# A state-space mixer and a LoRA feed-forward on one core: tiles of x and of turned rows wait for the products of their own place, and the first drive is made in halves

## The reference, cut to what matters

```python
proj = x @ W_in.T;  u, gate = split(proj)
u = silu(causal_conv4(u) + conv_b)
dt, B, C = split(u @ Wx.T);  dt, B, C = rmsnorm(each)
delta = softplus(dt @ Wdt.T + dt_bias)
state = exp(delta_t * A) * state + (delta_t * u_t) * B_t   # over t
y = sum_n(state * C_t) + u * D;   y = y * silu(gate)
x1 = layernorm(x + y @ W_out.T)
out = layernorm(x1 + x1 @ W.T + b + picked_lora(x1))
```

## Time and profile before

| what | before |
|---|---|
| median of 3 runs | 2262.96 us (2259.63 to 2263.5) |
| profiled execution, its own time | 2262.3 us |
| its span | 2260.5 us |
| TensorE busy | 2064.6 us, 91% |
| VectorE busy | 1994.2 us, 88% |
| GpSimd busy | 1819.4 us, 80% |
| ScalarE busy | 1481.8 us, 66% |
| granted TensorE clock, mean | 0.967 |

### The profile page before, as it was taken

The page is one execution under the profiler, slowest core; times in us unless marked ns, Lnnn a source line. Parts: engine busy times, 40 slices in busy tenths (PEclk is TensorE's granted clock), DMA queues, the critical chain, the costliest instruction groups (busy, mean ns, idle before and its releaser), DMA issues. The chain is left out here.

```text
span 2260.5 us, 30748 instructions
## 1 busy us (share of the span) xinstructions
PE 2064.6 (91%) x10528; PEld 1548.8 (69%) x10528; DVE 1994.2 (88%) x2403; ACT 1481.8 (66%) x2197; POOL 1819.4 (80%) x780
## 2 busy tenths in 40 slices
PE   8989689999999799999899997989989999897998
PEld 6867567777565477777775556868866556675577
DVE  4438899999999999999999999989989999999933
ACT  4478667777666677676886567675686566856521
POOL 4379888987999999778799988977688987699740
PEclk9989899999999999999999998999999999998999
DMA  4467556765332447655453333474453337443340
GB/s 153 137 214 238 198 199 232 226 206 181 92 119 82 131 148 234 233 190 166 137 190 113 111 97 97 152 261 154 148 181 115 108 94 224 154 156 127 102 141 38
DMA packets 168764, 354.84 MB, mean 157 GB/s; under 512 B 18656, under 2 KB 45408, under 8 KB 168608
## 3 DMA queue, kind: packets, MB, share of 16 engines
q1 hardware_dynamic: 168608, 352.87, 48.7%
HBM read 283.96 MB, written 68.85 MB: 156 GB/s over the span
## 5 line engine op out<-in xcount | busy, mean ns | idle before, releaser
L1544 POOL TENSOR_TENSOR drive<-delta_u,b_bcast 128x2048 f32<-128x2048 f32 x256 | 1172.1, 4582 | 106.9 <-PE state_t L916 98.7
L1098 DVE TENSOR_TENSOR_SCAN drive<-decay,drive 128x512 f32<-128x512 f32 x1024 | 1191.5, 1204 | 60.1 <-ACT decay L1338 34.7
L1338 ACT ACTIVATE decay<-delta,a_sb 128x512 f32<-128x512 f32 x1024 | 694.8, 688 | 416.0 <-DVE drive L1098 411.2
L916 PEld LDWEIGHTS state_t<-identity,drive 128*128 128x128 f32 x4096 | 485.5, 145 | 337.6 <-DVE drive L1098 148.6
L916 PE MATMUL state_t<-identity,drive 128*128 128x128 f32 x4096 | 592.1, 283 | 130.0 <-DVE drive L1098 96.1
L1106 DVE SCALAR_TENSOR_TENSOR y_acc<-state_t,c_rows,y_acc 128x512 f32<-128x512 f32 x724 | 513.2, 734 | 44.4 <-PE state_t L916 40.2
L947 PE MATMUL bank<-cols_high,w_split 128*128 128x512 f32 (+1 forms) x1240 | 523.5, 422 | 20.8 <-POOL w_split L1569 8.5
L949 PE MATMUL bank<-cols_high,w_split 128*128 128x512 f32 (+1 forms) x1240 | 491.0, 396 | 0.0
L948 PE MATMUL bank<-cols_low,w_split 128*128 128x512 f32 (+1 forms) x1240 | 489.0, 394 | 0.0
L970 PE MATMUL bank<-channels,w_raw 128*128 128x512 f32 x896 | 424.2, 597 | 1.3 <-POOL channels L1565 0.9
L1549 POOL TENSOR_TENSOR y_acc<-y_acc,scaled 128x512 f32<-128x512 f32 x236 | 303.0, 1284 | 120.6 <-ACT scaled L1358 118.8
(11 more groups left out here) (224 smaller groups left out, 1446.9 us busy)
## 6 DMA issues: line engine op xcount, KB each, us to landing
w_split<-w_split SPq DMA_DIRECT2D x272, 512.0 KB, 4.0
b_bcast<-b_rows SPq DMA_DIRECT2D x256, 256.0 KB, 3.5
w_raw<-in_w_out SPq DMA_DIRECT2D x112, 256.0 KB, 3.0
w_raw<-in_w_in SPq DMA_DIRECT2D x96, 256.0 KB, 4.3
gates<-scratch SPq DMA_DIRECT2D x64, 256.0 KB, 3.9
scratch<-gates SPq DMA_DIRECT2D x64, 256.0 KB, 4.7
rows<-in_x_rows SPq DMA_DIRECT2D x4, 2048.0 KB, 9.5
out<-rows SPq DMA_DIRECT2D x16, 512.0 KB, 4.6
```

The lines of the kernel that those rows point to most:

```text
L916: last = engine.transpose(bank[0:tile.shape[1], i * P:(i + 1) * P], tile, identity[:, :])
L1098: engine.tensor_tensor_scan(state, decay[(GT * s + t) % DECAYS][:, :], state, 0.0, ALU.mult, ALU.add).then_inc(signal["scan"])
L1338: engine.activation(decay[i % DECAYS][:, :], delta[:, g % 2, t, :], ACT.Exp, scale=a_sb[:, j, n:n + 1]).then_inc(signal["decay"])
L1544: engine.tensor_tensor(drive[key % DRIVES][:, :, :], du[:, :, :], row, ALU.mult).then_inc(signal["drive"])
```

## The change

It does four things. `products(b, k)` asks for place k of the 32 jobs alone, and `x1_job`, `load_x` and the waits of ScalarE use it with the tile's own k; for sequences 2 and 3 `x_high` needs `f_mm` of its own k in all eight jobs and, newly, `route_mm` of that k. The assumed duration of `x_first` in `load_x(1)` goes from 0.69 to 1.3 us. Drive 0 is made by two instructions of two tiles, `drive_begun` after the first half of `du`, `drive` after the second, and the scans of tiles 0 and 1 of unit 0 wait for the first of them alone. Everything else of the program is as before, but for the order that the plan gives.

```diff
+def drive_of(s, t):
+    return "drive" if s or t >= GT // 2 else "drive_begun", s
-    def products(b):
-        return [(stage, (b, j, HT - 1)) for stage in ("u_mm", "g_mm") for j in range(DT)]
+    def products(b, k):
+        return [(stage, (b, j, k)) for stage in ("u_mm", "g_mm") for j in range(DT)]
...
-        old = products(s + 1)
+        old = products(s + 1, h)
...
     def load_x(b, due):
-        old = [("f_mm", (b - 2, h, HT - 1)) for h in range(HT)] if b > 1 else products(0) if b else []
         for k in range(HT):
+            old = [("f_mm", (b - 2, h, k)) for h in range(HT)] + [("route_mm", (b - 2, 0, k))] if b > 1 else products(0, k) if b else []
...
-            put("POOL" if b > 1 else "DVE", due + 0.1 * k, 1.28 if b > 1 else 0.69, *low_of(b, k), [("x_high", (b, k))],
+            put("POOL" if b > 1 else "DVE", due + 0.1 * k, 1.28 if b > 1 else 1.3, *low_of(b, k), [("x_high", (b, k))],
...
-        put("POOL", q - 8, 4.56, "drive", s, [("fetch", s), ("du", (b, g, 1))] + (
+        if s == 0:
+            put("POOL", q - 8.2, 2.35, "drive_begun", s, [("fetch", s), ("du", (b, g, 0)), ("lora_rest", 0)] + [("x_first", (0, k)) for k in range(HT)])
+        put("POOL", q - 8, 4.56 if s else 2.35, "drive", s, [("fetch", s), ("du", (b, g, 1))] + ([] if s else [("drive_begun", 0)]) + (
...
-            put("DVE", i, 1.13, "scan", (s, t), [("drive", s), ("decay", (s, t))],
+            put("DVE", i, 1.13, "scan", (s, t), [drive_of(s, t), ("decay", (s, t))],
...
-                    e.wait_ge(*done("drive", s))
+                    e.wait_ge(*done(*drive_of(s, t)))
...
-                            e.wait_ge(*done("f_mm", (b - 2, h, HT - 1)))
+                            e.wait_ge(*done("f_mm", (b - 2, h, k)))
+                        e.wait_ge(*done("route_mm", (b - 2, 0, k)))
                     if b == 1:
-                        products_done(0)
+                        products_done(0, k)
...
-                    products_done(s + 1)
+                    products_done(s + 1, h)
...
-                if stage == "drive":
+                if stage in ("drive", "drive_begun"):
                     b, g, n = UNITS[key]
+                    tiles = slice(0, GT // 2) if stage == "drive_begun" else slice(0 if key else GT // 2, GT)
...
-                    e.wait_ge(*done("du", (b, g, 1)))
+                    e.wait_ge(*done("du", (b, g, 0 if stage == "drive_begun" else 1)))
...
-                    engine.tensor_tensor(drive[key % DRIVES][:, :, :], du[:, :, :], row, ALU.mult).then_inc(signal["drive"])
+                    engine.tensor_tensor(drive[key % DRIVES][:, tiles, :], du[:, tiles, :], row, ALU.mult).then_inc(signal[stage])
```

More of the change, by code:

```diff
@@ L1323, in scratch_of, with products_done @@
                 return scratch[place["scratch", holder]]
[L1325 to L1328, removed]
+            def products_done(b, k):
+                for stage in ("u_mm", "g_mm"):
+                    for j in range(DT):
+                        e.wait_ge(*done(stage, (b, j, k)))
             for _, stage, key in plan.work["ACT"]:
@@ L1531, in _ @@
             for _, stage, key in plan.work["POOL"]:
-                if stage == "drive":
+                if stage in ("drive", "drive_begun"):
                     b, g, n = UNITS[key]
-                    row = b_bcast[key % 2][:, :].unsqueeze(1).broadcast_to([P, GT, T])
+                    tiles = slice(0, GT // 2) if stage == "drive_begun" else slice(0 if key else GT // 2, GT)
+                    row = b_bcast[key % 2][:, :].unsqueeze(1).broadcast_to([P, tiles.stop - tiles.start, T])
                     e.wait_ge(*done("fetch", key))
-                    e.wait_ge(*done("du", (b, g, 1)))
+                    e.wait_ge(*done("du", (b, g, 0 if stage == "drive_begun" else 1)))
                     if key >= DRIVES:
```

## The result

The changed kernel takes 2271.73 us, the median of 7 runs (2269.09 to 2275.12); the kernel before, in runs beside it, 2262.32 (2259.63 to 2265.76). The ratio is 1.0043 with a 95% interval of 1.0033 to 1.0052: **9.4 us slower**. The profiled execution took 2273.07 us with a span of 2271.3, at a mean granted clock of 0.962 (before: 0.967).

What follows compares the result with a forecast made beforehand. VectorE and GpSimd set the pace up to 682 us, both nearly together with TensorE up to 1186, then TensorE. Terms -1.5 + 0 - 2 - 3 + 0 = -6.5 us gave 2255.8, as median 2256.5 us; range 2241 to 2272.

Steps and rivals of the forecast that it cites:

- the sum: Whole kernel: -1.5 + 0 - 2 - 3 + 0 = -6.5 us on the profiled 2262.3 us.
- moves only the order: Plan's price of x of sequence 1's low parts, now 1.3 us: said to change just the order; no term given.
- the low parts' new place: VectorE's eight low parts of x of sequence 1, moved earlier: 0 taken, between -8.2 and +17.3 us.
- Part one: First drive in halves at the start: drive 1 gains 0.7 to 2 us, 1.5 us carried to the end.
- Part two: x of sequence 1, waits by place: first product 4 to 8 us earlier, but 0 at the end.
- the first u product: Sign for sequence 1 on TensorE: starts at 295 to 299 us if the forecast is right.
- the first `x_high`: Sign for x of sequence 1: comes before 256 us if the forecast is right.
- The release at 682.26: Start of sequence 0's second-half output products: 1 to 2 us earlier; a move over 4 us means wrong.
- Part three: x of sequences 2 and 3, waits by place: gains of 2 us (0 to 2.2) and 3 us (0 to 6).
- Part four: Turned rows, waits by place: TensorE still runs the due products first; nothing gained, at best 2 us.
- The nearest rival: TensorE after 1186 us: a turn of states gets in front of ready products, +7.2 us, 2270 us; chance 0.16.
- The other slower rival: x of sequence 1: all eight low parts under drives, by the lock, +10.8 us, 2274 us; chance 0.07.

Runs made afterwards that it cites:

- e6: All edits of the changed kernel, queues in the order of the kernel before, first half drive put in by hand: 2259.18 us, ratio 0.9989.
- e5: Kernel before with only the assumed duration of a low part of x of sequence 1 at 1.3 instead of 0.69 us: 2268.95 us, ratio 1.0031.
- e12: Kernel before with the assumed duration of a low part of x of sequence 1 at 0.70 instead of 0.69 us: 2280.25 us, ratio 1.0075.
- e9: All edits of the changed kernel, queues in the order it gets without the half drive, half drive put in by hand: 2254.04 us, ratio 0.9963.
- e7: Kernel before with only the first drive in halves, put in by hand, order else that of before: 2259.88 us, ratio 0.9993.
- e2: Kernel before with only the first drive in halves, in the new order the plan gives: 2265.11 us, ratio 1.0010.
- e3: Kernel before with only the waits by place for x of sequences 2 and 3, in its own order: 2258.88 us, ratio 0.9981.
- e10: Kernel before with the assumed duration at 1.3 us and the pair of delta products behind sequence 0's turned rows: 2261.89 us, ratio 0.9998.
- e1: Changed kernel with one need more, putting the pair of delta products behind the turned rows of sequence 0: 2267.11 us, ratio 1.0019.

## Why the prediction was wrong

I forecast 2256.5 us and a gain; it is 2271.7 and a loss. The edits, taken by themselves, did roughly what the steps said or less; the failure is one assumption under all of them.

- **The step that failed** is in the sum: it has no term for the new order. I wrote that the price "moves only the order", as if that were nothing, took 0 for the low parts' new place, and priced every edit in the order of before. The queues are the output of `Plan.arrange`, and the new order is the largest term of all. In the order of before the edits gain 2.7 us (e6), in the one that the plan draws for them they lose 9.4, so this draw costs 12.1 us where I had put 0. The price alone, with no edit at all, costs 7.1 us (e5) and a hundredth of a microsecond 17.6 (e12), and another draw for the same edits gains 8.6 (e9).
- **Part one** (-1.5): the half drive's length was right, 2.40 us for 2.38. I had placed it in GpSimd's gap of 2.68 us; the plan put it behind du, and drive 1 gained 0.1 us. Put in the gap by hand it gives 1.2 us at drive 1 and 2.0 at the end, not told apart from none (e7). With its own order it costs 2.2 (e2). In the kernel after, the stretch from the first half of du to unit 4 even grew by 1.7 us.
- **Part two** (0): the first u product came at 299.71 us (I said 295 to 299), the first `x_high` at 259.2 (I said before 256); counted from unit 4 the u product is only 1.9 us earlier, where I had 4 to 8. The release at 682.26 moved by +6.6 us to 688.86, past the 4 us that I had named as the sign of an error. That what TensorE gains there is lost before 682 holds for TensorE alone; but the same place can move VectorE's recurrence either way: 7.8 us later at unit 16 in the kernel after, 5.5 earlier in e9.
- **Part three** (-2 and -3): near in sum, and partly by luck. Alone it gives 4.0 us (e3), none of it at sequence 2. And it gives them with an order of its own: in the order of before all waits by place together give 0.7 us (e6 against e7). In the kernel after, x of sequence 3 wins back 4.1 us (14.4 to 10.3 in the first table).
- **Part four** (0): as forecast, though no run has this edit alone. In the plan the need by place of the turned rows changes no piece of any queue.
- **The nearest rival** is the misplaced piece on TensorE's queue, at 0.16, with 2270 us against 2271.7. Its first sentence was right: the order on all engines is made anew, and the wrong piece can get in front in a strictly ordered queue. Its place and its piece were not: I looked for a turn of states after 1186 us, and here it was a pair of delta products at 790 us that held banks. After 1186 us TensorE's waits for VectorE's scans stayed: 36.2 us in the kernel after, 37.8 before. So that its number fits to 2 us is luck. In e12, 47.7 us, the waits that it spoke of did grow, by 9.9 us. The other slower rival, low parts under drives, was seen in the trace (three instead of two), and e10 shows that 7.9 us of it can vanish by the end.
- The range, 2241 to 2272, held the result at its very edge. That it held the result is luck too: it should have been as wide as the scatter of orders, 2254 to 2280 us here.

What is shown: what the plan makes anew is the cause (e5, e6, e9, e12), and about half of the loss goes with the pair ahead of the turned rows (e1), the order behind the pair included. What stays open: how much the stretched rows cost by themselves, how much of the rest the moved additions have in it, and which pieces make units 14 to 16 later. The low parts under drives are not the main reason there, by e2, e5, e10 and e12, though no run moves them alone. The traces put 13.4 us between the kernel after and e9 at unit 16, of which 6.0 are won back by unit 64.

## What to carry to other kernels

Where a program's order is made by a greedy planner, any edit, even one of a hundredth of a microsecond in an assumed duration, is two changes: its own and a new order. Time it in the kept order as well, and set the effect against the scatter of orders (here one set of edits took 2254 us in one order and 2272 in another, and the kernel without them 2262 and 2280), before you credit or blame the edit. The reverse holds as well: an edit that lets pieces start earlier may give nothing until the order uses it. Check too whether the planner decides more than the order, such as which engine does a piece. Then look for pieces that hold a scarce buffer while they wait for a slow reader: one such pair in front of eight short ones stretched them from 7.1 to 18.0 us, and a need that keeps it behind them is cheap. But don't book the whole stretch as loss: part of it is other work done early.

## What was not expected of the hardware

The start of an execution differs from run to run by more than some of these edits are worth. The first half of du, the same work in every kernel up to there, starts at 128.45 us in the kernel after, 131.69 before, 130.50 in e3 and 133.10 in e12, and what follows moves with it as long as the order is the same: from there to unit 4 it is 41.97 us before and in e3, and 41.98 in e12. With the half drive put in by hand the same stretch still differs between kernels with the same queues up to there, from 40.27 us (e6) to 41.26 (e9). E3's and e12's GpSimd timelines:

```profile
130.50 2.51 POOL L1565 TENSOR_TENSOR delta_u<-delta,channels 128x512 f32<-128x512 f32 x2 [3.41 <-ACT delta L1446]
```

```profile
133.10 2.52 POOL L1558 TENSOR_TENSOR delta_u<-delta,channels 128x512 f32<-128x512 f32 x2 [3.41 <-ACT delta L1440]
```

A step of 1 or 2 us can't be read from two traces' absolute times; count from a common piece behind the start.
